# Three of the eleven down-projection chunks as split float32r products, and four other orders at the end of the gated MLP

## The chip, the cores and the metric

The kernel runs on one core of one Trainium2 chip. The metric is the device time of one execution in microseconds (us). Before the change three runs gave a median of 681.93 us (681.78 to 682.07).

## The reference, cut to what matters

Four residual layers run over x, 4 batches of 256 tokens of 512 values: attention, a mixture of experts (MoE), a gated MLP, and the same MoE once more. The change lies in the MLP and in what leads from it to the second MoE.

```python
s = silu(x @ w_gate.T)                          # 1024 x 1376
_, idx = top_k(-abs(s), 688)                    # the smaller half of each row ...
s = s.at[rows, idx].set(0.0)                    # ... becomes zero
x = x + (s * (x @ w_up.T)) @ w_down.T           # "down": 1376 -> 512

# MoE: a router, two of three experts for each batch
ratio = mean(abs(h[:, 76:])) / (mean(abs(h[:, :76])) + 1e-8)
scores = softmax(concat([h, ratio]) @ gate_w + gate_b)
# experts are chosen by a batch's first token; each has w1, a function, w2
```

## The kernel before, in words

The tokens lie in T = 8 tiles of 128. Matrix products of float32 accuracy are mostly made of three float32r products: each factor is split into a high part (cast to F32R) and a low part (the rest), and high·high, high·low and low·high are summed in PSUM. The transposes, `down` and a few small products take plain float32 factors; each such product stands as two MATMUL records in the trace.

The order on each engine is that of the program, with semaphores in between (`need(engine, signal, step, k)` waits for the k-th event of a step). In the MLP, PE goes through iterations n = 0 to 7 (the loop at the end of the tensor block):

1. `up(n)`, 3 groups of columns of 12 products each (banks 3, 4, 5). After the first group comes `check(n)`, a product that counts the rows whose threshold search failed. It waits for DVE's search of tile n (`mlp.pick`) and for the add of tile n-1 (`mlp.y_add`), because its result lies in bank 7, the bank of `down`. In iteration T-3 = 5 `check` first issues `route_sums`, four small products for the router of the second MoE, on bank 7 too.
2. `turn_row(n+3)`, then `gate(n+2)` (36 products, banks 0 to 2).
3. `turn_product(n)`: 11 transposes of `mlp_prod` into banks 6, 4 and 3 (k = 0, 1, 2). Before k = 2 it waits for `mlp.prodT` 1, DVE's copy of k = 0.
4. `down(n)`: 11 chunks of 128 (the last of 96) rows of `w_down`, in bank 7, all float32.

In iteration 7 there is no gate; PE does `ffn_turn(ffn2, 0)` before `up(7)` and `ffn_front(ffn2, 0)` behind it. After `down(7)` it turns row 1 of the second MoE and runs `ffn_front(ffn2, 1)`: for each of two experts high·high, high·low, and then low·high, which waits for `hT_lo` from DVE (`ffn_low`).

DVE does in iteration n: `mlp_add(n-1)` (x += bank 7, then the norm's statistics); `keep_mask(n)`; `product(n)` (two parts into `mlp_prod`); `keep_product(n)` (copies bank by bank into `prodT`, lines 1627 to 1639); `search(n+1)`; router rows `logit_rows(n-1)`. The last iterations hold more: in T-3 the router's `take_sums`, `scores` and `ranks`; in T-2 two low parts of w1 (`weight_low`), `mlp_add(6)`, and the router's `weights` and `middle_weights`. After the loop come `mix` of tile 0, three low parts of w2 (`second_weights`), `mlp_add(7)`, and then `ffn_dve`, which begins with `ffn_low(ffn2, 1)`.

ACT computes silu, sizes and six counting passes per tile, and casts the high parts of w1 and w2. POOL computes the norms' factors and some low parts. In the trace w1 and w2 of the second MoE are both called `w_second`.

Of the kernel before, what the change touches and what calls it, by code (L numbers as in the profile page):

```python
# [162 lines left out]
def build(nc, x_in, w_attn, b_attn, w_proj, b_proj, w_gate, w_up, w_down,  # L163
# [26 lines left out]
    with ExitStack() as ctx:  # L190
# [26 lines left out]
        bias1 = sb("bias1", [P, E, D], BF16)  # L217
        bias_proj = sb("bias_proj", [P, D], BF16)
# [124 lines left out]
        assert at[0] <= arena + G_AT  # L343
        at[0] = past_hT
# [38 lines left out]
        assert at[0] <= arena + 2 * W  # L383
# [4 lines left out]
        def turned(n):  # L388
            if n % 3 == 2:
# [70 lines left out]
                         slow=sig("mlp_slow", SLOW), prodT_ps=sig("mlp_prodT_ps", 3), prodT=sig("mlp_prodT", 4),  # L460
# [7 lines left out]
        wg_end_high, wg_end_low = sem("wg_end_high"), sem("wg_end_low")  # L468
        out_done, first_silu, first_gate = sem("out_done"), sem("first_silu"), sem("first_gate")
# [284 lines left out]
        def _(act):  # L754
# [271 lines left out]
            second_weights(w2_second, 1)  # L1026
# [3 lines left out]
        def _(dve):  # L1030
# [521 lines left out]
            def keep_mask(n, then):  # L1552
# [4 lines left out]
                if then is not None:  # L1557
                    then()
# [84 lines left out]
            for c in range(KC):  # L1643
# [7 lines left out]
                                    ALU.subtract).then_inc(wu_low, 1)  # L1651
            router = Router(route2, 0, CHECK_BANK, 8)
            search(0)
            for n in range(T):
                if 1 <= n < T - 1:
                    mlp_add(n - 1)
                if n == T - 1:
                    ffn_low(ffn2, 0, HT_BANK)
                keep_mask(n, router.take_sums if n == T - 3 else None)
                product(n)  # L1660
                keep_product(n)
                if n == T - 2:
                    for e in range(1, E):
                        weight_low(w1_second, w1_high, w1_low, 1, e, e)
                if n + 1 < T:
                    search(n + 1)
                if n == T - 2:
                    mlp_add(n)
                if 1 <= n < T - 1:
                    logit_rows(route2, n - 1)  # L1670
                if n == T - 3:
                    router.scores()
                    router.ranks()
                elif n == T - 2:
                    router.weights()
                    router.middle_weights()
# [6 lines left out]
        def _(pe):  # L1683
# [479 lines left out]
```

## Time and profile before

| what | value |
|---|---|
| median of 3 runs | 681.93 us |
| the profiled execution, its own time | 681.57 us |
| its span, first to last instruction | 679.8 us |
| TensorE's granted clock over the span | 1.000 |
| PE busy | 641.1 us (94%) |
| DVE busy | 483.0 us (71%) |
| ACT busy | 343.7 us (51%) |
| POOL busy | 92.0 us (14%) |
| PE's share of the chain that ended last | 79% |
| the MLP's `up`, from its first product to the last `down` | about 366 to 576 us |

The table is of one profiled execution on the chip; the times are from its span's start. The 1.77 us between span and time lie before the first and behind the last instruction. In a timeline a row holds the start in us, the us from the first start to the last end of the merged instructions, engine, line, operation, output<-inputs, shapes and how many; in brackets the engine's idle time before it and what it waited for. A matmul's own duration is longer than the distance to the next one, since they are pipelined: what PE needs is read from start to start.

### The profile page before, as it was taken

The page shows a single profiled execution, that of the slowest core. Times are in us where ns is not written, and L with a number is a line of the kernel's source. Part 1 is how long each engine was busy: PE and PEld are TensorE (multiplying, and loading weights), DVE is VectorE, ACT ScalarE, POOL GpSimd, SP SyncE. Part 2 cuts the span into 40 slices and gives each one's busy share as a digit, 9 for nine tenths or more (in the row PEclk, how much of TensorE's full clock was granted, in tenths as well). Part 3 has the DMA queues.
Part 4 walks back from the last instruction along what each step waited for, and adds up shares of the span by engine and source line. Part 5 has one row for each costly group of instructions (what it writes and reads, how often), then busy time and mean ns, then how long its engine had stood idle before and what let it go on. Part 6 is the DMA issues. An engine that isn't in the chain of part 4 may idle for free.

```text
span 679.8 us, 10305 instructions
## 1 busy us (share of the span) xinstructions
PE 641.1 (94%) x3848; PEld 487.2 (72%) x3848; DVE 483.0 (71%) x921; ACT 343.7 (51%) x539; POOL 92.0 (14%) x185
## 2 busy tenths in 40 slices
PE   4878999999998999999999899999999999999997
PEld 4856678679676677887788576766857665788776
DVE  6755585796589889887697656365374898778556
ACT  5213544613633774522479997476483915434221
POOL 4411002102100121101042010000100350000000
PEclk9999999999999999999999999999999999999999
DMA  8395503322744331000161000000003106000000
GB/s 282 110 264 173 157 32 97 117 70 73 241 128 146 119 121 47 0 1 1 49 225 61 1 0 1 0 1 0 1 0 114 74 7 225 2 32 16 15 32 32
DMA packets 31908, 52.15 MB, mean 77 GB/s; under 512 B 3449, under 2 KB 17148, under 8 KB 30303
## 3 DMA queue, kind: packets, MB, share of 16 engines
q1 hardware_dynamic: 31282, 49.84, 22.6%
q10 hardware_dynamic: 576, 1.64, 1.0%
q8 instruction: 32, 0.52, 0.3%
q14 instruction: 18, 0.15, 0.1%
HBM read 42.87 MB, written 8.40 MB: 75 GB/s over the span
## 4 chain that ended last, share of the span: by engine, by line
PE 79%; DVE 12%; ACT 4%; DMA 1%; issue 1%; ACTq 1%; POOL 1%; SPq 0%; DVEq 0%; POOLq 0%
PE ps L2031 14%; PE ps L1900 13%; PE ps L1867 13%; PE ps L2100 10%; PE ps L1730 5%; DVE nmax L1099 3%; PE ps L1808 3%; PE ps L1746 2%; PE ps L1876 2%; PE ps L1798 2%; PE ps L1710 2%; DVE nmax L1096 2%; ACT sign_junk L988 1%; PE ps L1821 1%; PE ps L2089 1%
## 5 line engine op out<-in xcount | busy, mean ns | idle before, releaser
L2100 PE MATMUL ps<-wdT,prodT 128*128 128x512 f32 (+1 forms) x176 | 76.9, 592 | 0.0
L817 ACT ACTIVATE probsT<-ps 128x1536 f32<-128x1536 f32 x32 | 46.2, 1450 | 30.2 <-PE ps L1798 30.0
L2100 PEld LDWEIGHTS ps<-wdT,prodT 128*128 128x128 f32 (+1 forms) x176 | 32.8, 190 | 38.3 <-issue 38.3
L857 ACT ACTIVATE funs<-ps 128x512 f32<-128x512 f32 x16 | 9.5, 596 | 90.4 <-PE ps L1869 78.7
L683 POOL TENSOR_SCALAR ln_spread<-ln_moments 128x1 f32<-128x1 f32 x24 | 7.5, 311 | 272.1 <-DVE ln_moments L1171 271.9
L1633 DVE COPY prodT<-ps 128x512 f32<-128x512 f32 (+1 forms) x24 | 13.7, 599 | 41.3 <-PE ps L2089 41.0
L1177 DVE SCALAR_TENSOR_TENSOR junk<-x_sb,gate_row 128x512 f32<-128x512 f32 x48 | 41.2, 858 | 1.0
L1448 DVE SCALAR_TENSOR_TENSOR x_sb<-b_row,coef,x_sb 128x512 f32<-128x512 f32 x48 | 38.0, 792 | 1.8
L1099 DVE TENSOR_REDUCE nmax<-ps 128x4 f32<-128x1024 f32 x32 | 38.9, 1215 | 0.0
L988 ACT ACTIVATE sign_junk<-mlp_size_next,minus_guess 128x1376 bf16<-128x1376 f32 x24 | 34.6, 1443 | 0.8
L988 ACT ACTIVATE sign_junk<-mlp_size_main,minus_guess 128x1376 bf16<-128x1376 f32 x24 | 34.6, 1442 | 0.7
L918 ACT CAST aT_hi<-ps 128x512 fp32r<-128x512 f32 x32 | 17.2, 591 | 34.2 <-PE ps L1876 34.2
L676 POOL TENSOR_TENSOR parts<-resid,parts 128x512 bf16<-128x512 f32 x16 | 18.7, 1173 | 101.2 <-ACT parts L792 101.2
L785 ACT ACTIVATE parts<-ps,qk_bias 128x256 bf16<-128x256 f32 x32 | 13.4, 468 | 35.4 <-PE ps L1730 35.4
L1376 DVE TENSOR_TENSOR aT_lo<-ps,aT_hi 128x512 fp32r<-128x512 f32 x32 | 20.6, 684 | 12.7 <-ACT aT_hi L918 12.6
L1086 DVE SCALAR_TENSOR_TENSOR resid<-ps,qk_bias,parts 128x256 f32<-128x256 f32 x32 | 14.0, 479 | 21.8 <-ACT parts L785 21.8
L1128 DVE COPY outT<-ps 128x256 f32<-128x256 f32 x32 | 13.5, 423 | 22.4 <-PE ps L1813 22.4
L1798 PE MATMUL ps<-qst,kst 107*128 107x256 bf16 x128 | 24.5, 272 | 0.0
L1769 PE MATMUL ps<-kst,qst 104*128 104x256 bf16 x128 | 24.5, 272 | 0.0
L1730 PE MATMUL ps<-rowsT_hi,wqkv_hi 128*128 128x256 f32 x128 | 22.4, 299 | 2.1 <-DVE rowsT_lo L1053 1.4
L1457 DVE TENSOR_TENSOR x_sb<-ps,x_sb 128x512 f32<-128x512 f32 x16 | 11.1, 691 | 18.6 <-PE ps L1900 18.5
L1808 PE MATMUL ps<-probsT,v_ones 128*32 128x256 f32 x256 | 20.4, 391 | 3.7 <-DVE o_tok L1122 2.6
(302 smaller groups left out, 1726.4 us busy)
## 6 DMA issues: line engine op xcount, KB each, us to landing
cuts<-parts SPq DMA_DIRECT2D x16, 384.0 KB, 2.8
qst<-cuts SPq DMA_DIRECT2D x48, 128.0 KB, 2.6
w_first_raw<-in_L_ffn_w SPq DMA_DIRECT2D x6, 1024.0 KB, 7.6
w_second_raw<-in_L_ffn_w SPq DMA_DIRECT2D x6, 1024.0 KB, 8.5
kst<-cuts SPq DMA_DIRECT2D x36, 128.0 KB, 2.8
wqkv_raw<-in_L_attn_a_w_attn SPq DMA_DIRECT2D x3, 1024.0 KB, 8.0
wdT<-in_L_attn_b_w_down SPq DMA_DIRECT2D x1, 2560.0 KB, 9.9
wg_raw<-in_L_attn_b_w_gate SPq DMA_DIRECT2D x1, 2048.0 KB, 8.4
```

What stands on the lines that cost most here:

```text
L817: nc.scalar.activation(probsT[:, g % 2, :].rearrange("p (k n) -> p k n", k=3), slot[g % 2], ACT.Exp).then_inc(exp_ok.sem, 1)
L988: nc.scalar.activation(sign_junk[:, :], size_rows(n)[1][:, :], ACT.Sign, bias=minus_guess[:, i:i + 1], accum_out=probe_sum[:, i:i + 1]).th ...
L1099: nc.vector.tensor_reduce(nmax[:, 1, g * G:(g + 1) * G], sl[:, 1:3, :].rearrange("p s (h k) -> p (s h) k", h=2), AX.X, ALU.max, negate=Tru ...
L1177: nc.vector.scalar_tensor_tensor(out=junk[:, :], in0=x_sb[:, t, :], scalar=1.0, in1=gate_v[:, 0:D, e], op0=ALU.mult, op1=ALU.mult, accum_o ...
L1448: nc.vector.scalar_tensor_tensor(out=x, in0=b2_row[:, e, :], scalar=coef[:, n, e:e + 1], in1=x, op0=ALU.mult, op1=ALU.add).then_inc(ffn.b2 ...
L1730: last = nc.tensor.matmul(turn_bank(b, f)[:, m * S:(m + 1) * S], weight[:, side, c, columns], rows[:, c, :], start=(i == 0 and c == 0), st ...
L1798: m = nc.tensor.matmul(sl[:, 1 + i // 2, (i % 2) * S:(i % 2 + 1) * S], kst[0:MROWS, h, 0:P], qst[0:MROWS, h, :], start=False, stop=True, s ...
L1808: nc.tensor.matmul(o_ps[32 * i:32 * i + 2 * HD, 0:S], v_ones[:, 0, h, :], probsT[:, g % 2, D + i * S:D + (i + 1) * S], start=True, stop=Fa ...
L1867: nc.tensor.matmul(ps[:, 2 * i + s, :], a[:, i, c, :], part[:, e, c, :], start=(k == 0 and c == 0), stop=False)
L1900: last = nc.tensor.matmul(ps[:, Y_BANK, :], a[:, s, c, :], part[:, e[s], c, :], start=(k == 0 and c == 0), stop=(k == len(products) - 1 an ...
L2031: last = nc.tensor.matmul(ps[:, first_bank + q, 0:m], a[:, c, :], parts_of[c][part], start=(k == 0 and c == 0), stop=(k == 2 and c == KC - 1))
L2100: last = nc.tensor.matmul(ps[:, Y_BANK, :], prodT[0:m, c, :], wdT[0:m, c, :], start=(c == 0), stop=(c == IC - 1))
```

## The change

- **Down.** Chunks 5, 6 and 7 of 11 become three float32r products each: `prodT_hi`·`wd_hi`, `prodT_hi`·`wd_lo`, `prodT_low`·`wd_hi`. DVE splits the weights once, before `search(0)` (1536 columns). In every tile it splits the product: one cast and two subtractions in `split_product`, and the copy of bank 4 shrinks to chunk 4. The order of `down` becomes chunks 0 to 3, then 5 to 7, then 4, then 8 to 10.
- **The transposes' wait.** `turn_product` waits before k = 2 for `mlp.prod` 2 (both parts of the product) in place of `mlp.prodT` 1.
- **The router's sums** leave `check` and come behind `up(5)`, ahead of `gate(7)`. DVE takes them, and does `scores` and `ranks`, between `product(5)` and `keep_product(5)`.
- **DVE's end.** In iteration 6 the two low parts of w1 come behind `search(7)`, with `mlp_add(6)` between them; `logit_rows(5)` moves into iteration 7, ahead of `keep_product(7)`; `weights` and `middle_weights` come after `keep_product(7)`.
- **ACT** waits for `wd_read` (`down(7)`'s last float32r product) before the cast of w2's third expert, whose place `wd_hi` uses.

```diff
+        prodT_hi = sb("prodT_hi", [P, NSPLIT, P], F32R, prodT_at + 4 * SPLIT.start * P)
+        wd_at = arena + LATE + W - 4 * IC * D
+        wdT = sb("wdT", [P, IC, D], F32, wd_at)
+        wd_lo = sb("wd_lo", [P, NSPLIT, D], F32R, wd_at + 4 * SPLIT.start * D)
+        wd_hi = sb("wd_hi", [P, NSPLIT, D], F32R, wd_at - 4 * NSPLIT * D)
...
-            second_weights(w2_second, 1)
+            second_weights(w2_second, 1, range(E - 1))
+            act.wait_ge(wd_read, 1)
+            second_weights(w2_second, 1, (E - 1,))
...
+            def split_product(n, chunks_ps):
+                nc.vector.tensor_copy(prodT_hi[:, :, :], chunks_ps).then_inc(mlp.prodT.sem, 1)
+                need(dve, mlp.prodT, n, 2)
+                for low, part in zip(prodT_low, (slice(0, NSPLIT - 1), slice(NSPLIT - 1, NSPLIT))):
+                    nc.vector.tensor_tensor(low[:, :, :], chunks_ps[:, part, :], prodT_hi[:, part, :].bitcast(F32),
+                                            ALU.subtract).then_inc(mlp.prodT.sem, 1)
...
+                    if k == 1:
+                        split_product(n, turned_ps[:, SPLIT.start - 4:SPLIT.stop - 4, :])
+                        chunks = SPLIT.start - 4
...
+            dve.wait_ge(wd_here, 32)
+            nc.vector.tensor_copy(wd_hi[:, :, :], wdT[:, SPLIT, :]).then_inc(wd_high, 1)
+            dve.wait_ge(wd_high, 1)
+            nc.vector.tensor_tensor(wd_lo[:, :, :], wdT[:, SPLIT, :], wd_hi[:, :, :].bitcast(F32),
+                                    ALU.subtract).then_inc(wd_low, 1)
...
-                keep_mask(n, router.take_sums if n == T - 3 else None)
+                keep_mask(n)
                 product(n)
+                if n == T - 3:
+                    router.take_sums()
+                    router.scores()
+                    router.ranks()
+                elif n == T - 1:
+                    logit_rows(route2, T - 3)
                 keep_product(n)
-                if n == T - 2:
-                    for e in range(1, E):
-                        weight_low(w1_second, w1_high, w1_low, 1, e, e)
                 if n + 1 < T:
                     search(n + 1)
-                if n == T - 2:
+                if 1 <= n < T - 2:
+                    logit_rows(route2, n - 1)
+                elif n == T - 2:
+                    weight_low(w1_second, w1_high, w1_low, 1, 1, 1)
                     mlp_add(n)
-                if 1 <= n < T - 1:
-                    logit_rows(route2, n - 1)
-                if n == T - 3:
-                    router.scores()
-                    router.ranks()
-                elif n == T - 2:
-                    router.weights()
-                    router.middle_weights()
+                    weight_low(w1_second, w1_high, w1_low, 1, 2, 2)
+            router.weights()
+            router.middle_weights()
             mix(ffn2, route2, 0, 0)
...
-                if n == T - 3:
-                    route_sums(route2, 0, CHECK_BANK, 8)
...
-                        need(pe, mlp.prodT, n, 1)
+                        need(pe, mlp.prod, n, 2)
...
-                for c in range(IC):
+                for c in range(4):
+                    if c == 0:
+                        need(pe, mlp.prodT, n, 1)
+                    nc.tensor.matmul(ps[:, Y_BANK, :], prodT[:, c, :], wdT[:, c, :], start=(c == 0), stop=False)
+                if n == 0:
+                    pe.wait_ge(wd_low, 1)
+                need(pe, mlp.prodT, n, 4)
+                for k in range(NSPLIT):
+                    high, low = prodT_hi[:, k, :], prodT_low[k // (NSPLIT - 1)][:, k % (NSPLIT - 1), :]
+                    for a, w in ((high, wd_hi), (high, wd_lo), (low, wd_hi)):
+                        last = nc.tensor.matmul(ps[:, Y_BANK, :], a, w[:, k, :], start=False, stop=False)
+                if n == T - 1:
+                    last.then_inc(wd_read, 1)
+                for c in [*range(4, SPLIT.start), *range(SPLIT.stop, IC)]:
...
                 up(n)
+                if n == T - 3:
+                    need(pe, mlp.mask, n, 1)
+                    route_sums(route2, 0, CHECK_BANK, 8)
```

PE at the end of a tile, here of tile 4 (`mlp_prod` is transposed, then `down`). Before:

```order
L2089 MATMUL ps<-ident,mlp_prod 128x128 x10
L2089 MATMUL ps<-ident,mlp_prod 96x128
L2100 MATMUL ps<-wdT,prodT 128x512 x11
L2031 MATMUL ps<-wu_hi,hT_hi_third 128x512 x4
L2031 MATMUL ps<-wu_lo,hT_hi_third 128x512 x4
L2031 MATMUL ps<-wu_hi,hT_lo_third 128x512 x4
```

With the change (`prodT_low_162` and `prodT_low_175` are the two low parts of the product; "..." leaves out a triple that reads as the one above it):

```order
L2118 MATMUL ps<-ident,mlp_prod 128x128 x10
L2118 MATMUL ps<-ident,mlp_prod 96x128
L2126 MATMUL ps<-wdT,prodT 128x512 x4
L2133 MATMUL ps<-wd_hi,prodT_hi 128x512
L2133 MATMUL ps<-wd_lo,prodT_hi 128x512
L2133 MATMUL ps<-wd_hi,prodT_low_162 128x512
...
L2133 MATMUL ps<-wd_hi,prodT_hi 128x512
L2133 MATMUL ps<-wd_lo,prodT_hi 128x512
L2133 MATMUL ps<-wd_hi,prodT_low_175 128x512
L2144 MATMUL ps<-wdT,prodT 128x512 x4
```

Seven float32 chunks are left of eleven, and nine float32r products stand between chunk 3 and chunk 4.

PE in `up(5)`, behind its first group of columns. Before:

```order
L2031 MATMUL ps<-wu_hi,hT_lo_third 128x512 x4
L1832 MATMUL ps<-abs_n,vision 128x2
L1833 MATMUL ps<-abs_n,text 128x2
L1835 MATMUL ps<-abs_n,ones_78 128x2
L1837 MATMUL ps<-logits_n,first_row 128x6
L2067 MATMUL ps<-ones_78,failed 1x1
L2031 MATMUL ps<-wu_hi,hT_hi_third 128x512 x4
L2031 MATMUL ps<-wu_lo,hT_hi_third 128x512 x4
L2031 MATMUL ps<-wu_hi,hT_lo_third 128x512 x4
```

With the change:

```order
L2062 MATMUL ps<-wu_hi,hT_lo_third 128x512 x4
L2096 MATMUL ps<-ones_78,failed 1x1
L2062 MATMUL ps<-wu_hi,hT_hi_third 128x512 x4
L2062 MATMUL ps<-wu_lo,hT_hi_third 128x512 x4
L2062 MATMUL ps<-wu_hi,hT_lo_third 128x512 x4
L2062 MATMUL ps<-wu_end_hi,hT_hi_third 128x352 x4
L2062 MATMUL ps<-wu_end_lo,hT_hi_third 128x352 x4
L2062 MATMUL ps<-wu_end_hi,hT_lo_third 128x352 x4
L1863 MATMUL ps<-abs_n,vision 128x2
L1864 MATMUL ps<-abs_n,text 128x2
L1866 MATMUL ps<-abs_n,ones_78 128x2
L1868 MATMUL ps<-logits_n,first_row 128x6
```

The four products of the router (`abs_n`, `logits_n`) now follow the last product of `up` and precede `gate(7)`; `check` (`failed`) follows the first group directly.

DVE from the last copy of tile 7 into the second MoE. Before:

```order
L1638 COPY prodT<-ps 96x128
L1421 TENSOR_SCALAR funs<-funs,coef_mid 128x512
L1424 SCALAR_TENSOR_TENSOR act_tok<-funs,coef 128x512
L1382 TENSOR_TENSOR w_second_lo<-w_second_raw,w_second_hi 128x2048 x3
L1623 TENSOR_TENSOR x_sb<-ps,x_sb 128x512
L1169 BN_STATS ln_stats<-x_sb 128x6
L1171 BN_AGGR ln_moments<-ln_stats 128x2
L1376 TENSOR_TENSOR hT_lo<-ps,hT_hi 128x512
```

With the change ("..." leaves out eleven more instructions of the router's `weights`):

```order
L1663 COPY prodT<-ps 96x128
L1360 TENSOR_REDUCE tiny<-tiny 128x4
...
L1385 TENSOR_TENSOR coef<-coef,tiny 128x12
L1387 TENSOR_TENSOR coef_mid<-coef,tiny 128x4 x2
L1390 TENSOR_SCALAR coef_half<-coef 128x4
L1438 TENSOR_SCALAR funs<-funs,coef_mid 128x512
L1441 SCALAR_TENSOR_TENSOR act_tok<-funs,coef 128x512
L1399 TENSOR_TENSOR w_second_lo<-w_second_raw,w_second_hi 128x2048 x3
L1638 TENSOR_TENSOR x_sb<-ps,x_sb 128x512
L1186 BN_STATS ln_stats<-x_sb 128x6
L1188 BN_AGGR ln_moments<-ln_stats 128x2
L1393 TENSOR_TENSOR hT_lo<-ps,hT_hi 128x512
```

The router's weights stand behind the last copies and ahead of the mix, the low parts of w2, the last add and `hT_lo` of row 1.

## Rows read from the trace of the kernel before

**Rows 1.** The chain that ended last on the page, its shares of the span by line
```profile
PE ps L2031 14%; PE ps L1900 13%; PE ps L1867 13%; PE ps L2100 10%; PE ps L1730 5%; DVE nmax L1099 3%; PE ps L1808 3%; PE ps L1746 2%; PE ps L1876 2%; PE ps L1798 2%; PE ps L1710 2%; DVE nmax L1096 2%; ACT sign_junk L988 1%; PE ps L1821 1%; PE ps L2089 1%
```

**Rows 2.** Timeline of PE, tile 1's product turned, its down, up of tile 2: start us, us, instructions
```profile
410.92 1.04 PE L2089 MATMUL ps<-ident,mlp_prod 128*128 128x128 f32 x8
412.31 0.55 PE L2089 MATMUL ps<-ident,mlp_prod 128*128 128x128 f32 x3 [0.35 <-DVE prodT L1633]
412.69 9.61 PE L2100 MATMUL ps<-wdT,prodT 128*128 128x512 f32 x22
...
423.07 1.07 PE L2031 MATMUL ps<-wu_lo,hT_hi_third 128*128 128x512 f32 x4
423.97 1.07 PE L2031 MATMUL ps<-wu_hi,hT_lo_third 128*128 128x512 f32 x4
424.97 0.19 PE L2067 MATMUL ps<-ones,failed 128*1 128x1 f32 x2
...
426.13 1.08 PE L2031 MATMUL ps<-wu_lo,hT_hi_third 128*128 128x512 f32 x4
```

**Rows 3.** Timeline of DVE in the same stretch
```profile
411.56 1.75 DVE L1633 COPY prodT<-ps 128x512 f32<-128x512 f32 x3 [7.86 <-PE ps L2089]
...
413.43 0.14 DVE L1538 TENSOR_SCALAR ladder<-minus_guess 128x1 f32<-128x1 f32 x1
...
421.88 0.09 DVE L1177 DVE_READ_ACCUMULATOR junk<-x_sb,gate_row 128x1 f32 x1
422.33 0.69 DVE L1623 TENSOR_TENSOR x_sb<-ps,x_sb 128x512 f32<-128x512 f32 x1 [0.37 <-PE ps L2100]
...
430.10 0.52 DVE L1574 TENSOR_TENSOR mlp_prod<-mlp_s_next,ps 128x352 f32<-128x352 f32 x1 [0.61 <-PE ps L2031]
```

**Rows 4.** Timeline of DVE before the first search
```profile
373.08 0.15 DVE L1538 TENSOR_SCALAR ladder<-minus_guess 128x1 f32<-128x1 f32 x1 [4.78 <-ACT sign_junk L988]
```

**Rows 5.** The tile wdT: its first load (issue at us) and both loads' times to landing
```profile
L613 SPq DMA_DIRECT2D wdT<-in_L_attn_b_w_down x1: 368/368/368, 350.0 to 350.0; - x1
...
DMA to landing us min/median/max: 9.9/10.0/10.1
```

**Rows 6.** Timeline of PE, up of tile T-3 = 5
```profile
504.74 1.07 PE L2031 MATMUL ps<-wu_hi,hT_lo_third 128*128 128x512 f32 x4
506.53 0.35 PE L1832 MATMUL ps<-abs_n,vision 128*128 128x2 f32 x2 [0.72 <-POOL logits_n L700]
...
507.49 0.19 PE L2067 MATMUL ps<-ones,failed 128*1 128x1 f32 x2
```

**Rows 7.** Timeline of PE, up of tile T-2 = 6, and its down's start
```profile
532.97 1.07 PE L2031 MATMUL ps<-wu_hi,hT_lo 128*128 128x512 f32 x4
534.35 0.19 PE L2067 MATMUL ps<-ones,failed 128*1 128x1 f32 x2 [0.32 <-DVE x_sb L1623]
...
541.29 9.61 PE L2100 MATMUL ps<-wdT,prodT 128*128 128x512 f32 x22
```

**Rows 8.** Timeline of DVE, tiles 6 and 7 into the second MoE
```profile
556.99 0.15 DVE L1343 TENSOR_REDUCE tiny<-tiny 128x4 f32<-128x12 f32 x1
...
559.32 0.68 DVE L1376 TENSOR_TENSOR hT_lo<-ps,hT_hi 128x512 fp32r<-128x512 f32 x1
...
567.51 0.47 DVE L1421 TENSOR_SCALAR funs<-funs,coef_mid 128x512 f32<-128x512 f32 x1
...
568.68 2.28 DVE L1382 TENSOR_TENSOR w_second_lo<-w_second_raw,w_second_hi 128x2048 fp32r<-128x2048 f32 x1
...
576.41 0.69 DVE L1623 TENSOR_TENSOR x_sb<-ps,x_sb 128x512 f32<-128x512 f32 x1 [0.15 <-PE ps L2100]
...
577.97 0.66 DVE L1376 TENSOR_TENSOR hT_lo<-ps,hT_hi 128x512 fp32r<-128x512 f32 x1
```

**Rows 9.** Timeline of ACT, the third cast of the second w2
```profile
572.04 1.90 ACT L845 CAST w_second_hi<-w_second_raw 128x2048 fp32r<-128x2048 f32 x1 [0.76 <-DMA w_second_raw<-in_L_ffn_w]
```

**Rows 10.** Timeline of PE, second MoE, front of tile 1, its third product
```profile
579.45 1.10 PE L1867 MATMUL ps<-w_second_hi,hT_lo 128*128 x4
```

More of the change, by code:

```diff
@@ L217, in build @@
         bias1 = sb("bias1", [P, E, D], BF16)
+        bias_proj_at = at[0]
         bias_proj = sb("bias_proj", [P, D], BF16)
@@ L343, in build @@
         assert at[0] <= arena + G_AT
+        SPLIT = slice(5, 8)
+        NSPLIT = SPLIT.stop - SPLIT.start
         at[0] = past_hT
@@ L350, in build @@
         mlp_flag = sb("mlp_flag", [P, I], BF16)
+        prodT_at = at[0]
         prodT = sb("prodT", [P, IC, P], F32)
+        prodT_hi = sb("prodT_hi", [P, NSPLIT, P], F32R, prodT_at + 4 * SPLIT.start * P)
+        prodT_low = [sb("prodT_low0", [P, NSPLIT - 1, P], F32R)]
         assert at[0] <= arena + G_AT, at[0] - arena - G_AT
@@ L368, in build @@
         wu_end_hi = sb("wu_end_hi", [P, KC, IT], F32R, b2_at)
+        prodT_low.append(sb("prodT_low1", [P, 1, P], F32R, bias_proj_at))
         wu_hi = sb("wu_hi", wide_shape, F32R, arena + W)
-        wdT = sb("wdT", [P, IC, D], F32, arena + LATE)
+        wd_at = arena + LATE + W - 4 * IC * D
+        wdT = sb("wdT", [P, IC, D], F32, wd_at)
+        wd_lo = sb("wd_lo", [P, NSPLIT, D], F32R, wd_at + 4 * SPLIT.start * D)
+        wd_hi = sb("wd_hi", [P, NSPLIT, D], F32R, wd_at - 4 * NSPLIT * D)
+        assert SPLIT.start > 4 and SPLIT.stop == 8
         assert MAIN + TAIL + 4 * IT <= W and 4 * IC * D <= W and TAIL <= 4 * E * D
@@ L382, in build @@
         hT_lo_third = sb("hT_lo_third", [P, KC, P], F32R)
-        assert at[0] <= arena + 2 * W
+        assert at[0] <= wd_at - 4 * NSPLIT * D
         def size_rows(n):
@@ L459, in build @@
                          pick=sig("mlp_pick", 7), check=sig("mlp_check", 1), mask=sig("mlp_mask", 2), prod=sig("mlp_prod", 2),
-                         slow=sig("mlp_slow", SLOW), prodT_ps=sig("mlp_prodT_ps", 3), prodT=sig("mlp_prodT", 4),
+                         slow=sig("mlp_slow", SLOW), prodT_ps=sig("mlp_prodT_ps", 3), prodT=sig("mlp_prodT", 7),
                          y_ps=sig("mlp_y_ps", 1), y_add=sig("mlp_y_add", 1))
@@ L468, in build @@
         wg_end_high, wg_end_low = sem("wg_end_high"), sem("wg_end_low")
+        wd_high, wd_low, wd_read = sem("wd_high"), sem("wd_low"), sem("wd_read")
         out_done, first_silu, first_gate = sem("out_done"), sem("first_silu"), sem("first_gate")
@@ L1550, in search, with keep_mask @@
                 link(nc.vector.tensor_scalar(failed[:, :], cut_count[:, :], float(KEEP), None, ALU.not_equal))
-            def keep_mask(n, then):
+            def keep_mask(n):
                 rows, size = size_rows(n)
@@ L1556, in keep_mask @@
                 nc.vector.tensor_copy(failures[0:1, :], check_ps).then_inc(mlp.mask.sem, 1)
-                if then is not None:
-                    then()
                 need(dve, mlp.mask, n, 1)
@@ L1632, in keep_product @@
                         chunks -= 1
-                    nc.vector.tensor_copy(prodT[:, 4 * k:4 * k + chunks, :],
-                                          ps[:, PROD_BANK[k], 0:chunks * P].rearrange("p (c t) -> p c t", t=P)
+                    turned_ps = ps[:, PROD_BANK[k], :].rearrange("p (c t) -> p c t", t=P)
+                    if k == 1:
+                        split_product(n, turned_ps[:, SPLIT.start - 4:SPLIT.stop - 4, :])
+                        chunks = SPLIT.start - 4
+                    nc.vector.tensor_copy(prodT[:, 4 * k:4 * k + chunks, :], turned_ps[:, 0:chunks, :]
                                           ).then_inc(mlp.prodT.sem, 1)
@@ L2093, in down @@
             def down(n):
-                for c in range(IC):
+                for c in range(4):
[12 more added lines that the diff above has]
+                for c in [*range(4, SPLIT.start), *range(SPLIT.stop, IC)]:
                     m = min(P, I - c * P)
-                    if c % 4 == 0:
-                        need(pe, mlp.prodT, n, c // 4 + 1)
+                    if c == 4:
+                        need(pe, mlp.prodT, n, 5)
+                    elif c == SPLIT.stop:
+                        need(pe, mlp.prodT, n, 6)
                     elif c == IC - 1:
-                        need(pe, mlp.prodT, n, 4)
+                        need(pe, mlp.prodT, n, 7)
                     last = nc.tensor.matmul(ps[:, Y_BANK, :], prodT[0:m, c, :], wdT[0:m, c, :],
-                                            start=(c == 0), stop=(c == IC - 1))
+                                            start=False, stop=(c == IC - 1))
                 last.then_inc(mlp.y_ps.sem, 1)
```

## The prediction

> **What bounds the kernel now.** I read the page's chain first: PE's lines lead it, and L2031 (`up` and `gate`), L2100 (`down`) and L2089 (the transposes) are 25% of the span [rows 1]. So the MLP is timed by PE, and the questions are how much PE time goes, and whether another engine then comes late. For that I went through PE's timeline tile by tile, then DVE's beside it, then ACT and the loads where a wait is added. PE does not stand still in a middle tile but for two gaps: one inside the transposes, for DVE's copy [rows 2], and one of about 0.1 us ahead of `check`.
>
> **1. Down, three chunks in float32r.** A float32 chunk is two passes. From the first pass of `down` at 412.69 to the `wu_lo` products at 423.07 lie 22 passes and four float32r products [rows 2]. Four of those take 0.90 us (423.07 to 423.97), 0.225 each. So 10.38 - 0.90 = 9.48 us for 22 passes: 0.43 each, 0.86 a chunk. Three chunks cost 2.58 us, nine float32r products 2.03 to 2.07. Saved: **0.52 us a tile**. The switch from float32 to float32r inside that stretch leaves nothing over; the switch back I also take at nothing.
>
> The Trainium skill, page "TensorE: Matmul & The Clock Gate", section "Back-to-back issue gap", gives a sustained 131 ns for each 512-column matmul in a stream with weight loads. This trace has 225. By the page nine products would be 1.18 us and the saving 1.40 a tile; I go by the row.
>
> **2. The transposes' wait.** Before, PE waits at 412.31 for the copy of k = 0, then does three transposes, and `down` starts at 412.69 [rows 2]. After, these three fill the gap: eight transposes take 0.87 (11 in all about 1.2 us, to 412.1), and `down` starts when the same copy is there, at 412.31. Saved: 412.69 - 412.31 = **0.38 us a tile**. `mlp.prod` 2 has long come: DVE makes it before PE's 36 products of `gate`.
>
> So a tile is 0.90 us shorter. That holds for tiles 0 to 5 and 7: 7 x 0.90 = **6.3 us**.
>
> **3. DVE's additional work in each tile.** Before, `keep_product` takes 413.43 - 411.56 = 1.87 us with four instructions [rows 3]. After there are seven: widths 512, 384, 256, 128, 128, 256, 128. A one-column operation takes 0.14 [rows 3], a 512-column one from PSUM 0.66 [rows 8], so 0.14 + 0.001 a column: the four new pieces (384, 256, 128, 128) are 0.53 + 0.40 + 0.27 + 0.27 less the 0.66 that goes, some 0.07 less for each overlap, 0.05 more for the wait of the low parts on the cast: **+0.65 us**. Bounds: +0.4 (the columns alone), and +2.9, if each of the four took 0.69 and a wait of its own. I take 0.65, since the copies in the same rows show the overlap.
>
> Is it covered? Count from the first copy, S = 411.56. DVE is free of its router rows at 421.97 = S + 10.4 [rows 3]; then it adds (0.69), which `check` waits for. After: S + 11.05 + 0.7 = S + 11.8. PE issued `check` at 424.97 = S + 13.4 [rows 2], after at S + 12.5. 0.7 us are left, so nothing is lost in tiles 2 to 6. PE reaches chunk 5 some 3.4 us into `down`, when the split (S + 1.8) has been over for 2 us or more.
>
> The split of the weights (1536 columns, at most two operations of 1.7 us by the 2.28 of a 2048-column one [rows 8]) stands ahead of `search(0)`, where DVE idles for 4.78 us waiting for ACT [rows 4]. Its data, issued at 350.0, land 10 us later [rows 5], before that idle time starts at 368.3. Cost 0; without this cover it would be up to 3.4 us, once.
>
> **4. The router's sums.** Before, the last products ahead of `check` in tile 5 start at 504.74, so `check` could go at 505.74 (1.00 us later, as 423.97 to 424.97 [rows 2]); it goes at 507.49, having waited 0.72 us for POOL and issued four small products [rows 6]: 1.75 us lost. After, POOL has been done for some 3 us when PE comes to them, and they cost 507.49 - 506.53 = 0.96 plus 0.1 to start. DVE's scores and ranks fall into its idle time before the transposes (7.86 us in such a tile [rows 3]). Saved: **0.7 us** (bounds 0.5 and 0.9).
>
> **5. Tile 6.** `check(6)` waited for the add of tile 5, as DVE was late with scores and ranks: it went at 534.35 and could have gone at 532.97 + 1.00 = 533.97 [rows 7]. Saved 0.38. From `check` to `down` were 541.29 - 534.35 = 6.94 us, as there is no `gate` between. After: DVE's second part of the product starts 430.10 - 424.97 = 5.13 us after a `check` [rows 2, 3], 0.44 later comes the copy of k = 0 (0.69), then `down`: 6.3 us. Saved 0.6. With the 0.52 of part 1: **1.5 us**.
>
> **6. The end of DVE, a new wait.** From S = 567.51 - 1.87 = 565.64, tile 7's first copy, DVE now does: `keep_product` 1.87 + 0.65 = 2.5; the router's weights 559.32 - 556.99 = 2.3; the mix 568.68 - 567.51 = 1.2; three low parts of w2 at 2.28 each, 6.8; the add and statistics 577.97 - 576.41 = 1.6; `hT_lo` of row 1, 0.66 [rows 8]. Its end: S + 15.1. Before, PE used `hT_lo` at 579.45 = S + 13.8 [rows 10]; with PE 0.90 ahead it wants it at S + 12.9. So **PE waits 2.1 us**, in order, in `ffn_front(ffn2, 1)`, and nothing behind it makes that up. Bounds: 1.3 (the low parts overlap, the rest is short) and 3.0 (the split costs more).
>
> ACT's wait for `wd_read`: the third cast starts at 572.04 and waited for its load until then [rows 9]. `down(7)` passes its last float32r product 0.69 + 3.4 + 2.1 = 6.2 us after S, at 571.9 in the old times: level with the load, cost 0 to 0.3 on ACT, covered by DVE's other low parts.
>
> In tile 6 DVE does only one low part of w1 ahead of the add instead of two; PE's `check(7)` finds the add done about 1 us earlier. 0.
>
> **Sum:** 6.3 + 0.7 + 1.5 - 2.1 = 6.4 us. From the profiled execution's 681.57: 675.2. The median of the runs is 0.36 above that execution; I predict **675.5 us**, its own range 674.5 to 676.6. A measurement of this kernel tells about 0.2% (1.4 us) from no change.
>
> **Rivals.**
> - **No wait at the end** (or a short one): the 2.1 us rest on a sum of DVE pieces. If they overlap more, or PE gets to `ffn_front(ffn2, 1)` later, the whole 8.5 us stay: 673.4. Against it: the router's 2.3 us are new in this row of work, and before it DVE had only 0.8 us to spare.
> - **Switches between float32 and float32r cost.** `check` is two float32 passes among float32r ones: 423.97 to 426.13 is 2.16 us for eight products, 1.80 without it [rows 2]. Some 0.3 us, of which the passes are 0.05. `down` gets one more pair of switches a tile: at most 8 x 0.25 = 2.0 us, 677.5. Against it: the wait for a semaphore explains part, and the first switch in part 1 shows none.
> - **DVE becomes the bound, slower.** `check(n)` waits for the add, the add for DVE's row of copies, search and router rows. Past +1.35 us (0.65 + 0.7) each further us counts in five to six tiles and again at the end. At the bound of +2.9 that is 1.55 x 6 = 9.3 and 2.3 at the end: 675.5 + 11.6 = 687. It decides for slower from about +2.5 on. For it: four more instructions, each with a fixed part. Against it: the overlap in rows 3.
> - **Products at half the distance.** Were two float32r products to overlap as they stream, each would take half of the 0.225 of rows 2; the nine would be 1.0 us and 1.0 us a tile more would go: 675.5 - 8.1 = 667.4. Every float32r product of 512 columns in this trace speaks against it. The rule of the Trainium skill in part 1 is of this kind.
>
> **How the numbers follow.** Forecast 0.68; no or a short wait at the end 0.13; switches 0.12; DVE as the bound 0.03; half the distance 0.01; something unseen that takes most of the gain 0.03. The range of 8 in 10 takes in the second and most of the third: 673.2 to 677.4. Faster by over 0.2%: all but the fourth and the last, 0.94; within 0.2%: 0.03; slower: 0.03.
>
> **What would show it.** In the timeline of PE after: the transposes x11 without idle time; nine products at 0.23 us between the float32 passes; `down` 0.5 us shorter; tile to tile 26.0 instead of 26.9 us; no wait at `check(6)`; and, in the front of row 1 of the second MoE, an idle time of about 2 us ahead of its third product, released by DVE `hT_lo`. Wrong would be: a wait of `check` for `x_sb` in tiles 2 to 5, float32 passes that start late behind the float32r ones, or no idle time at `hT_lo`.

## The result and the profile after

| | before | after |
|---|---|---|
| median of the runs | 682.00 us (681.78 to 683.65, 6 runs) | 676.70 us (676.22 to 679.00, 6 runs) |
| ratio, 95% interval | | 0.9921 (0.9904 to 0.9937) |
| the profiled execution | 681.57 us, span 679.8 | 678.16 us, span 676.4 |
| granted clock over its span | 1.000 | 0.995 |

The kernel is 5.3 us faster. The forecast was 675.5 us, its range 673.2 to 677.4. The one execution of the six whose granted clock was 1.000 took 676.22 us; the profiled one spent two stretches at a lower clock (one in the attention stage, one in the second MoE), and the trace lets us take the second out.

Timeline of PE after, tile 1, the place of [rows 2]:

```profile
410.55 1.36 PE L2118 MATMUL ps<-ident,mlp_prod 128*128 128x128 f32 x11
411.93 3.70 PE L2126 MATMUL ps<-wdT,prodT 128*128 128x512 f32 x8
415.07 0.80 PE L2133 MATMUL ps<-wd_hi,prodT_hi 128*128 128x512 f32 x1
415.70 0.40 PE L2133 MATMUL ps<-wd_lo,prodT_hi 128*128 128x512 f32 x1
...
417.34 0.40 PE L2133 MATMUL ps<-wd_hi,prodT_low 128*128 128x512 f32 x1
417.57 3.60 PE L2144 MATMUL ps<-wdT,prodT 128*128 128x512 f32 x8
420.61 1.49 PE L2062 MATMUL ps<-wu_hi,hT_hi_third 128*128 128x512 f32 x4
421.94 1.07 PE L2062 MATMUL ps<-wu_lo,hT_hi_third 128*128 128x512 f32 x4
...
423.84 0.19 PE L2096 MATMUL ps<-ones,failed 128*1 128x1 f32 x2
```

The transposes stand as x11 with no idle time, and the float32r products follow one another at 0.234 us (415.70 to 417.34, seven steps). From the first transpose to `wu_lo` it is 421.94 - 410.55 = 11.39 us; before it was 423.07 - 410.92 = 12.15 [rows 2]. A tile is 0.76 us shorter, not 0.90.

Timeline of DVE after, the same tile:

```profile
411.18 0.69 DVE L1659 COPY prodT<-ps 128x512 f32<-128x512 f32 x1 [7.86 <-PE ps L2118]
411.79 0.55 DVE L1643 CAST prodT_hi<-ps 128x384 fp32r<-128x384 f32 x1
412.37 0.62 DVE L1646 TENSOR_TENSOR prodT_low<-ps,prodT_hi 128x256 fp32r<-128x256 f32 x2
...
413.64 0.14 DVE L1555 TENSOR_SCALAR ladder<-minus_guess 128x1 f32<-128x1 f32 x1
...
422.07 0.68 DVE L1638 TENSOR_TENSOR x_sb<-ps,x_sb 128x512 f32<-128x512 f32 x1
```

`keep_product` takes 413.64 - 411.18 = 2.46 us, 0.59 more than the 1.87 of [rows 3]. The add ends at 422.75, `check` is issued at 423.84: it waits for nothing, with 1.1 us to spare.

PE in tiles 5 and 6, the places of [rows 6] and [rows 7]:

```profile
501.35 1.07 PE L2062 MATMUL ps<-wu_hi,hT_lo_third 128*128 128x512 f32 x4
502.35 0.19 PE L2096 MATMUL ps<-ones,failed 128*1 128x1 f32 x2
...
507.29 0.28 PE L1863 MATMUL ps<-abs_n,vision 128*128 128x2 f32 x2
...
508.09 1.18 PE L2062 MATMUL ps<-wg_hi,hT_hi 128*128 128x512 f32 x4
...
529.00 0.19 PE L2096 MATMUL ps<-ones,failed 128*1 128x1 f32 x2
...
535.32 1.13 PE L2126 MATMUL ps<-wdT,prodT 128*128 128x512 f32 x2
```

Both checks go 1.00 us behind the group ahead of them (in tile 6 that group starts at 528.00); the router's products cost 0.80 us at 507.29, with no wait for POOL; `down(6)` begins 6.32 us after `check(6)`.

PE behind `down(7)`, the place of [rows 10]:

```profile
569.12 0.60 PE L1877 MATMUL ps<-ident,h_cur 128*128 128x128 f32 x4
570.39 1.20 PE L1898 MATMUL ps<-w_second_hi,hT_hi 128*128 x4 [0.68 <-ACT hT_hi L864]
571.43 1.09 PE L1898 MATMUL ps<-w_second_lo,hT_hi 128*128 x4
574.32 1.20 PE L1898 MATMUL ps<-w_second_hi,hT_lo 128*128 x4 [1.79 <-DVE hT_lo L1393]
...
575.40 2.02 PE L1898 MATMUL ps<-w_second_hi,hT_hi 128*128 x4
577.22 1.91 PE L1898 MATMUL ps<-w_second_lo,hT_hi 128*128 x4
578.93 1.17 PE L1898 MATMUL ps<-w_second_hi,hT_lo 128*128 x4
...
580.17 1.04 PE L1907 MATMUL ps<-ident,act_tok 128*128 128x128 f32 x8
```

The predicted wait is there: the third group starts 2.89 us after the second, where it was 0.93. But two groups behind it need 1.82 and 1.71 us in place of 1.13 and 0.92. The windows of PE show why (stretch, its length, PE busy, the granted clock, DMA):

```profile
574.30:575.40 1.10, 1.08 (x5) 1.00 0.00 0
575.40:578.90 3.50, 3.50 (x10) 0.54 0.00 0
578.90:582.40 3.50, 3.50 (x21) 0.97 0.00 0
...
575.60:575.70 0.10, 0.10 (x2) 0.88 0.00 0
...
579.00:579.10 0.10, 0.10 (x2) 0.55 0.00 0
```

The granted clock fell to half (of the two levels, 1.2 GHz) at 575.7, 1.4 us after PE had resumed at 574.32, and came back at 579.0, some 3.4 us later. DVE's end, for [rows 8]:

```profile
559.29 0.69 DVE L1659 COPY prodT<-ps 128x512 f32<-128x512 f32 x1 [2.27 <-PE ps L2118]
...
565.45 6.69 DVE L1399 TENSOR_TENSOR w_second_lo<-w_second_raw,w_second_hi 128x2048 fp32r<-128x2048 f32 x3
572.06 0.69 DVE L1638 TENSOR_TENSOR x_sb<-ps,x_sb 128x512 f32<-128x512 f32 x1
...
573.61 0.66 DVE L1393 TENSOR_TENSOR hT_lo<-ps,hT_hi 128x512 fp32r<-128x512 f32 x1
```

From the first copy (S = 559.29) to `hT_lo` the timeline marks no idle time of DVE.

**Where the 3.4 us between the two spans come from.** Three marks in each PE timeline: the first transpose of tile 0's product (384.00 before, 384.37 after), that of tile 7's (565.00, 558.65) and the first transpose of `act_tok` (583.64, 580.17).

| stretch | before | after | difference |
|---|---|---|---|
| span's start to tile 0's transposes | 384.00 | 384.37 | +0.37 |
| to tile 7's transposes | 181.00 | 174.28 | -6.72 |
| `down(7)`, to the transposes of row 1 | 11.22 | 10.47 | -0.75 |
| row 1's front, to `act_tok` | 7.42 | 11.05 | +3.63 |
| to the end of the span | 96.16 | 96.23 | +0.07 |

The +3.63 are 9.50 - 7.42 = 2.08 for the wait and 11.05 - 9.50 = 1.55 for the low clock: in another execution of the same code (r_after, below), whose groups behind the wait keep their usual distances, this stretch is 9.50 us.

### The profile page after: what moved, and what is told of

Read it like the earlier page. It is cut to its first block, busy times and chain, and to the rows that moved or that the text cites. A ratio compares the mean times of both kernels' runs of the same rounds, so it can differ in the third digit from the quotient of the medians.

```text
span 676.4 us, 10382 instructions
## 1 busy us (share of the span) xinstructions
PE 640.8 (95%) x3872; PEld 493.7 (73%) x3872; DVE 490.3 (72%) x947; ACT 343.9 (51%) x539; POOL 89.2 (13%) x185
## 3 DMA queue, kind: packets, MB, share of 16 engines
q10 hardware_dynamic: 576, 1.64, 1.1%
## 4 chain that ended last, share of the span: by engine, by line
PE 79%; DVE 12%; ACT 4%; DMA 2%; ACTq 1%; issue 1%; POOL 1%; SPq 0%; DVEq 0%
PE ps L2062 15%; PE ps L1931 13%; PE ps L1898 13%; PE ps L2126 4%; PE ps L1761 4%; PE ps L2144 4%; DVE nmax L1116 3%; PE ps L1839 3%; PE ps L1777 2%; PE ps L2133 2%; PE ps L1907 2%; PE ps L1829 2%; PE ps L1741 2%; DVE nmax L1113 2%; ACT sign_junk L1003 1%; PE ps L2118 1%
## 5 line engine op out<-in xcount | busy, mean ns | idle before, releaser
L698 POOL TENSOR_SCALAR ln_spread<-ln_moments 128x1 f32<-128x1 f32 x24 | 9.0, 373 | 271.4 <-DVE ln_moments L1188 271.3
L1659 DVE COPY prodT<-ps 128x512 f32<-128x512 f32 (+2 forms) x24 | 10.4, 462 | 39.4 <-PE ps L2118 39.4
L2126 PE MATMUL ps<-wdT,prodT 128*128 128x512 f32 x64 | 29.6, 605 | 0.2
L2144 PE MATMUL ps<-wdT,prodT 128*128 128x512 f32 (+1 forms) x64 | 28.8, 592 | 0.0
```

What stands on the lines that cost most here:

```text
L2126: nc.tensor.matmul(ps[:, Y_BANK, :], prodT[:, c, :], wdT[:, c, :], start=(c == 0), stop=False)
```

## The experiments

The yardstick is the **MLP stretch**, from the first transpose of tile 0's product to that of `act_tok`, read in each profile, beside the **tile period**, from one tile's first transpose to the next (median of the first four). They leave out the attention stage, whose clock differs from execution to execution.

| kernel | median us | ratio to before | tile period | MLP stretch |
|---|---|---|---|---|
| before | 682.00 | | 26.92 | 199.64 |
| after | 676.70 | 0.9921 (0.9904 to 0.9937) | 26.17 | 195.80 (1.6 of it low clock) |
| e1_wait | 680.99 | 0.9981 (0.9972 to 0.9990) | 26.64 | 198.52 |
| e2_orders | 679.75 | 0.9961 (0.9947 to 0.9975) | 26.64 | 196.78 |
| e3_end | 674.96 | 0.9895 (0.9880 to 0.9911) | 26.17 | 192.16 |
| e4_last | 678.12 | 0.9942 (0.9928 to 0.9955) | 26.15 | 194.10 |
| r_after | 678.07 | 0.9943 (0.9929 to 0.9957) | 26.17 | 194.23 |
| r_end | 675.21 | 0.9891 (0.9876 to 0.9906) | 26.17 | 192.17 |
| e9_turn | 673.64 | 0.9882 (0.9864 to 0.9899) | 26.17 | 191.42 |
| e8_dve4 | 691.69 | 1.0138 (1.0116 to 1.0160) | 28.2 | 208.46 |
| e6_two | 677.91 | 0.9932 (0.9909 to 0.9954) | 26.32 | 195.17 |
| e7_dve1 | 676.65 | 0.9920 (0.9897 to 0.9943) | 26.17 | 194.22 |
| e10_route | 678.78 | 0.9950 (0.9932 to 0.9968) | 26.17 | 195.88 |

Rows e1 to e4, r_after to e8, and e6 to e10 are three sets on chips of their own, where the kernel before took 682.46, 681.89 and 681.89 us. The ratio of a row is to the kernel before on its own chip.

**The transposes' wait alone, in the kernel before.**

```diff
-                        need(pe, mlp.prodT, n, 1)
+                        need(pe, mlp.prod, n, 2)
```

> The kernel before, with only the transposes' wait changed (mlp.prod 2 instead of mlp.prodT 1). Theory: the last three transposes fill the 0.38 us between the copy being asked for and being there, in each of 8 tiles: 682.0 - 3.0 = 679.0 us, and the transposes stand as x11 without idle time. Rival: the wait only moves ahead of the first product of down, which waits for the same copy: 682.0 us.

Measured: the stretch is 1.12 us shorter, not 3.0. PE at tile 1, and the checks of tiles 6 and 7:

```profile
411.07 1.36 PE L2089 MATMUL ps<-ident,mlp_prod 128*128 128x128 f32 x11
412.45 9.71 PE L2100 MATMUL ps<-wdT,prodT 128*128 128x512 f32 x22
...
533.24 0.19 PE L2067 MATMUL ps<-ones,failed 128*1 128x1 f32 x2 [0.48 <-DVE x_sb L1623]
...
553.66 0.19 PE L2067 MATMUL ps<-ones,failed 128*1 128x1 f32 x2 [0.96 <-DVE x_sb L1623]
```

`down` starts 1.38 us behind the first transpose instead of 1.77, as predicted, but then takes 0.10 longer: in tile 7 it is 9.54 us to the next transposes where it was 9.45. So the period shrinks by 0.28, not 0.38. And 1.1 of the 2.2 us that eight tiles bring are lost at once to DVE, which is late with the adds of tiles 5 and 6: `check(7)` waits 0.96 us where it did not wait before. The other orders of the change are what cashes the gain (next run).

**The orders without the split.** All eleven chunks in float32, no `split_product`, no split of the weights.

```diff
-                need(pe, mlp.prodT, n, 4)
-                for k in range(NSPLIT):
-                    high, low = prodT_hi[:, k, :], prodT_low[k // (NSPLIT - 1)][:, k % (NSPLIT - 1), :]
-                    for a, w in ((high, wd_hi), (high, wd_lo), (low, wd_hi)):
...
+                for c in range(IC):
+                    m = min(P, I - c * P)
+                    if c % 4 == 0:
+                        need(pe, mlp.prodT, n, c // 4 + 1)
```

> The changed kernel with all eleven chunks of down in float32 and no split; the orders and the transposes' wait stay. Theory: in the trace of the changed kernel the split takes 9.08 us per down where it was 9.45, so 0.37 us a tile and 3.0 in all come back. At the end of the MLP DVE has 0.6 us less to do and PE arrives 0.37 later, so the wait for hT_lo shrinks from 1.96 to about 1.0: 676.7 + 3.0 - 1.0 = 678.7 us; 677.2 if the 1.5 us lost to the lower clock behind that wait go too. Rival (the term as predicted, 0.52 a tile): 676.7 + 4.2 - 1.1 = 679.8 us.

Measured: a period of 26.64, so three split chunks save 26.64 - 26.17 = **0.47 us a tile**, between the theory's 0.37 and the 0.52 of the prediction. (The 0.37 came from comparing `down` with that of before, whose transposes end earlier.) The wait for `hT_lo` is shorter, as expected:

```profile
575.78 1.10 PE L1888 MATMUL ps<-w_second_lo,hT_hi 128*128 x4
577.49 1.20 PE L1888 MATMUL ps<-w_second_hi,hT_lo 128*128 x4 [0.60 <-DVE hT_lo L1391]
```

It costs 8.31 - 7.42 = 0.89 us. Against the changed kernel the stretch is 2.55 us longer (194.23 to 196.78): 8 x 0.47 = 3.76 come back, 1.18 of wait go. Against e1_wait the orders alone, of the router and of DVE together, are worth 198.52 - 196.78 = 1.74 us.

**DVE's end in another order** (and once more as r_end, beside the changed kernel as r_after).

```diff
-            second_weights(w2_second, 1)
+            for e in range(E - 1):
+                weight_low(w2_second, w2_high, w2_low, 1, e, e)
             mlp_add(T - 1)
+            ffn_low(ffn2, 1, HT_BANK)
+            weight_low(w2_second, w2_high, w2_low, 1, E - 1, E - 1)
```

> The changed kernel with hT_lo of row 1 and the last add ahead of the third low part of w2 on DVE. Theory: the wait of 1.96 us for hT_lo goes, and with it the stretch at the lower clock behind it, which cost 1.5 us in the profiled run: 676.7 - 3.5 = 673.2 us. If the lower clock has nothing to do with the idle time: 674.7 us, and the stretch is still to be seen in some runs. Rival: another wait takes its place in row 1 or 2 of the second MoE (the mix of row 1 or the third low part comes late): 676.7 us.

> The changed kernel with hT_lo of row 1 and the last add ahead of the third low part of w2, once more, beside the changed kernel on the same chip. Theory: 2.1 us of wait are gone, 674.6 us against 676.7; and if the lower clock behind the wait is a consequence of the wait, fewer of its runs than of the changed kernel's have a clock below 0.997. Rival: the difference on the first chip was the chip, and here it is under 1 us.

> The changed kernel once more, for a time beside the next three on one chip. All theories: 676.7 us, 676.2 where the granted clock stays 1.000, with a wait of 1.8 us for hT_lo in row 1.

Measured: the stretch is 192.16 and 192.17 against 194.23, 2.07 us less. The wait is gone and nothing took its place:

```profile
571.50 1.08 PE L1901 MATMUL ps<-w_second_lo,hT_hi 128*128 x4
572.43 1.09 PE L1901 MATMUL ps<-w_second_hi,hT_lo 128*128 x4
```

On the one chip the medians differ by 678.07 - 675.21 = 2.9 us. So the wait cost 2.07 us, and the time it cost was on the path. The part on the clock is not settled: in 2 of the 4 runs of r_end and in 4 of the 5 of r_after the mean clock was below 0.997, which is too few to tell them apart.

The expectation for r_after failed: its median is 678.07 us, not 676.7. Its one execution at a mean clock of 0.997 took 676.60, the four at 0.995 or 0.992 took 678.04 to 678.76. The profiles show what such a mean is made of: no stretch at the lower level at 1.000, one at 0.997 (in the attention stage in all of them), two at 0.995 (`after`), three at 0.993 (e8_dve4). So the median of one and the same kernel moves by over 1 us with the share of its executions in which the clock falls more than once. The MLP stretch of a single profile does not have this spread.

**The float32r products last.** In tiles 0 to 6, chunks 0 to 4 and 8 to 10 first, then the nine products, right ahead of `up`.

```diff
+                    singles(rest)
+                    last = triples()
```

> The changed kernel with the nine float32r products at the end of down (tiles 0 to 6), right ahead of up's float32r products, so that one pair of switches between float32 and float32r a tile goes. Theory: the switches cost the 0.1 us a tile that is left when nine products at 0.233 and eight passes at 0.43 are taken from the measured stretch: 676.7 - 0.7 = 676.0 us. Rival 1, switches are free: 676.7 us. Rival 2, a switch costs the 0.4 us that the first product behind the float32 passes stands longer in the trace: 676.7 - 2.8 = 673.9 us.

Measured: a period of 26.15 against 26.17. One pair of switches a tile fewer brings 0.02 us, not the theory's 0.1 and not the 0.4 of rival 2: **the switches cost nothing that shows**.

```profile
418.29 0.80 PE L2140 MATMUL ps<-wd_hi,prodT_hi 128*128 128x512 f32 x1
418.93 0.39 PE L2140 MATMUL ps<-wd_lo,prodT_hi 128*128 128x512 f32 x1
...
420.79 1.08 PE L2062 MATMUL ps<-wu_hi,hT_hi_third 128*128 128x512 f32 x4
421.70 1.07 PE L2062 MATMUL ps<-wu_lo,hT_hi_third 128*128 128x512 f32 x4
```

The `wu_hi` group now takes 0.91 us instead of 1.33, but the eight passes that were between the products and it have only moved ahead of them. So the extra 0.4 us of a first float32r product (0.63 in tile 1's rows, 0.64 here) is no loss; most likely it is recorded while the float32 pass ahead of it still runs. The median of 678.12 says nothing against it; its five executions had mean clocks of 1.000 (676.26 us), 0.995 (three) and 0.992 (679.15).

**Two split chunks instead of three.**

```diff
-        SPLIT = slice(5, 8)
+        SPLIT = slice(6, 8)
```

> The changed kernel with two split chunks (6 and 7) instead of three. The trace gives 26.64 us a tile without a split and 26.17 with three chunks. Theory (a gain per chunk, no fixed price of the switches): two thirds of 0.47, so 26.33 us a tile, 0.16 x 8 = 1.3 us less gain, of which DVE's shorter work (0.13) and PE's later arrival (0.16) give 0.3 back at the end: 677.7 us. Rival (a fixed price of 0.1 us a tile in each down, 0.19 us a chunk): 26.36 us a tile.

Measured: a period of 26.32. Each split chunk is worth 0.16 us (0.32 for two, 0.47 for three), and a fixed part, if there is one, is within the 0.02 to 0.03 us that rounding leaves.

**More work on DVE**, by one and by four idle reductions in each of tiles 0 to 5:

```diff
+                    for k in range(4):
+                        dve.wait_ge(spare_ok, 4 * n + k)
+                        nc.vector.tensor_reduce(spare[:, 0:4], x_sb[:, T - 1, :].rearrange("p (a b) -> p a b", a=4), AX.X,
+                                                ALU.add).then_inc(spare_ok, 1)
```

> The changed kernel with one idle reduction of 512 columns more on DVE in each of tiles 0 to 5, 0.7 us a tile. Theory (1.0 us to spare ahead of check): nothing, 26.17 us a tile and the time of the changed kernel, 676.7 us. Rival (every us on DVE in this row counts): 26.9 us a tile, 681 us.

> The changed kernel with four idle reductions of 512 columns more on DVE in each of tiles 0 to 5, about 2.6 us a tile. Theory (check waits for the add, with 1.0 us to spare in the trace of the changed kernel): checks 2 to 6 wait 1.6 us each for x_sb, 8 us in all: 684.7 us, and tile 1 waits for nothing, as it has no router rows. Rival (DVE's row has more slack than the add shows): 676.7 us.

Measured: one (0.69 us of record, 0.6 in the row of work) costs nothing, the period stays at 26.17. Four make every check of tiles 1 to 6 wait. PE in tile 3, and its clock there:

```profile
455.72 0.19 PE L2103 MATMUL ps<-ones,failed 128*1 128x1 f32 x2 [1.72 <-DVE x_sb L1640]
...
456.88 1.51 PE L2069 MATMUL ps<-wu_lo,hT_hi 128*128 128x512 f32 x4
458.18 1.91 PE L2069 MATMUL ps<-wu_hi,hT_lo 128*128 128x512 f32 x4
```

```profile
455.70:457.00 1.30, 1.28 (x7) 1.00 0.05 13
457.00:460.50 3.50, 3.50 (x12) 0.55 0.00 0
```

The four move the router rows by 2.76 us and the undisturbed period grows by 27.93 - 26.17 = 1.76: if each us past the reserve counts in full, the reserve is **1.0 us**. The timeline of the changed kernel gives the same by itself: 1.1 us between the end of the add and `check`. The expected 8 us became 14.2. Tile 1 waits too (its period grows by 1.9): it has no router rows, but its search starts late, behind a wait of 2.60 us for ACT. Behind two of the six waits the clock fell to the lower level, 1.6 us each time. And the five expected waits lengthen their periods by 1.75 to 2.07 us each instead of 1.6, which is the last 1.1.

**The router's products back ahead of `check(5)`.**

```diff
+                if n == T - 3:
+                    route_sums(route2, 0, CHECK_BANK, 8)
                 nc.tensor.matmul(check_ps, failed[:, :], ones32[:, 0:1], start=True, stop=True,
...
-                    need(pe, mlp.mask, n, 1)
-                    route_sums(route2, 0, CHECK_BANK, 8)
```

> The changed kernel with the router's four products back ahead of check(5); DVE's order stays as changed. Theory (the predicted term of 0.7 us for POOL's late logits_n): 0.7 to 0.8 us more in tile 5, whose period is 26.64 us now: 27.4 us and 677.4 us in all. Rival (POOL is no longer late in this order, or DVE's order made the gain): 26.64 us and 676.7.

Measured: tile 5 takes 28.29 us instead of 26.65, 1.64 more, and the stretch 195.88 against 194.22 (e7_dve1, whose period is that of the changed kernel, on the same chip).

```profile
501.06 1.07 PE L2062 MATMUL ps<-wu_hi,hT_lo_third 128*128 128x512 f32 x4
503.69 0.35 PE L1863 MATMUL ps<-abs_n,vision 128*128 128x2 f32 x2 [1.56 <-POOL logits_n L715]
```

The direction is the theory's, the size twice it. PE could now issue them at 502.06 (1.00 behind the group at 501.06) where it was 505.74 before, 3.7 us earlier; POOL is only 2.8 us earlier (503.69 against 506.53 [rows 6]), so the wait has grown from 0.72 to 1.56. Without this move 0.84 of the 3.7 us gained by then would have been given back here.

**Row 1's transposes inside `down(7)`**, on top of e3_end, and `hT_lo` ahead of the last add. Bank 6 is free there, since `down` itself waited for DVE's copy of it.

```diff
+                    if n == T - 1 and c == SPLIT.stop:
+                        ffn_turn(ffn2, 1, HT_BANK)
```

> As the run before this one, and the four transposes of row 1 stand inside the last down, ahead of chunk 8, with hT_lo ahead of the last add. Theory: PE waits 0.68 us for ACT's cast of hT_hi behind these transposes in every kernel so far; with 1.3 us of down behind them the cast is hidden: 0.7 us less than the run before. Rival: hT_lo or the functions of row 0 on ACT come late in its place: no difference.

Measured: 0.75 us less in the stretch (191.42), and the timeline marks no idle time of PE any more between tile 0's transposes and `act_tok`:

```profile
566.49 0.60 PE L1880 MATMUL ps<-ident,h_cur 128*128 128x128 f32 x4
566.92 2.74 PE L2149 MATMUL ps<-wdT,prodT 128*128 128x512 f32 x6
569.62 1.17 PE L1901 MATMUL ps<-w_second_hi,hT_hi 128*128 x4
...
571.56 1.10 PE L1901 MATMUL ps<-w_second_hi,hT_lo 128*128 x4
```

At 673.64 us this kernel is below both r_end (675.21) and the changed kernel (r_after, 4.4 us more) on the same chip.

## Why the prediction was right, and where it was off

| step of the prediction | predicted | measured |
|---|---|---|
| 1. down, three chunks in float32r | 0.52 a tile | 0.47 (e2_orders against after) |
| 2. the transposes' wait | 0.38 a tile | 0.28 (e1_wait against before) |
| both, tiles 0 to 5 and 7 | 6.3 | 7 x 0.75 = 5.25 |
| 3. DVE's additional work | +0.65, hidden | +0.59, hidden; 1.0 in reserve |
| 4. the router's sums | 0.7 | 1.30 - 0.47 = 0.83 (excess of tile 5's period) |
| 5. tile 6 | 1.5 | 1.39 (what is left of its two periods) |
| 6. the wait for `hT_lo` | 2.1 | 2.07 |
| sum | 6.4 | 5.4 |

The measured 5.4 are the stretch's 199.64 - 194.23. From the 681.57 us of the profiled execution they lead to 676.2, and the run at clock 1.000 took 676.22. So every mechanism was there. The saving was put 1.0 us too high, and 1.05 of that is in one place, with small ones beside it that nearly cancel.

**The step that failed is the pair 1 and 2**, 0.75 us a tile instead of 0.90. In part 2 I took what `down` starts earlier for what is saved. But when all eleven transposes run directly ahead of `down`, its 22 passes take 9.55 us to the next work, not 9.45 (e1_wait, e2_orders). That the transposes' end and `down`'s start overlap is the likely reason, but only argued; the 0.10 is measured. In part 1 nine products take 9 x 0.234 = 2.10 us where I had 2.03 to 2.07, which is most of the missing 0.05. By the rule of the Trainium skill, page "TensorE: Matmul & The Clock Gate", section "Back-to-back issue gap" (131 ns for a 512-column product in a stream with weight loads), the saving would have been 1.40 a tile, an estimate; the traces differ from it, with 0.234 us for such a product and 0.47 a tile.

**Tile 6** is 0.11 below its term. Its two waits gave what was predicted: 0.38, since `check(6)` now goes 1.00 us behind its group instead of 1.38, and 0.62, since `down(6)` begins 6.32 us behind it instead of 6.94. The 0.10 of the transposes is the likely rest. **The router's term** was larger by 0.13; e10_route shows that by itself it is not a constant: it is worth 0.83 against the kernel before and 1.64 inside the change.

**The wait at the end** came out at 2.07, and not by luck: from S to the end of `hT_lo` are 574.27 - 559.29 = 14.98 us (15.1 in the sum), and PE wanted it at S + 13.07 (12.9), 0.93 behind its second group. Of the pieces of the sum none is off by more than 0.2: the router's weights took 2.5 (2.3 predicted), the three low parts of w2 6.6 (6.8). The two ends give 1.91 and the groups' distance 1.96; the remaining 0.1 of the 2.07 is lost behind the wait, and no run shows where. ACT's wait for `wd_read` cost nothing, as its cast at 566.99 waited 2.13 us for the load.

**The rivals.** No wait at the end: fell, the wait was there. Costly switches: fell, by e4_last and e6_two. DVE as the bound: its price was right in kind (e8_dve4), but it starts from a dose of 1.0 us beyond the changed kernel's work, and the change stays below. Products at half the distance: fell, 0.234 us each.

**What I did not foresee** is the clock. In the profiled execution it fell behind the wait, and with this 1.6 us and 0.4 more ahead of the MLP the execution gained only 3.4 us. That the wait brought it about is not shown.

**Where luck had a part.** That the median fell inside the range also rests on how seldom the clock fell in these six executions, of which two had a mean below 0.997. The same kernel on another chip (r_after, four of five below 0.997) had a median of 678.07 us, 3.8 us below the kernel before there (681.89) and above the range of 673.2 to 677.4. The range had no term for this.

## What to carry to other kernels

Read the worth of a removed wait from start to start over a whole period, not from the start of the next instruction; here 0.38 was 0.28. Price every wait against the state after the other parts (the router's was worth 0.83 us before and 1.64 inside the change): a part that makes PE earlier makes each producer that stays where it is (POOL's `logits_n`, DVE's adds and `hT_lo`) later in comparison, so that orders which save little alone decide how much of the gain arrives. And when work is added to an engine's closing row, look for what in it is needed last: one low part of w2, ready at 572 us and not used before 585, stood ahead of `hT_lo`. With that part behind it (e3_end, r_end) the 2.07 us came back.

## What the runs showed of the hardware

The granted clock fell to its lower level in the middle of steady work, shortly after PE had stood still for 1.7 to 1.8 us: once in the profile of the changed kernel and twice in that of e8_dve4, 1.1 to 1.6 us after PE had resumed, for some 3.4 us, at a price of about 1.6 us each. It did not do so behind waits of the same length in the profiles of r_after, e4_last, e7_dve1 and e10_route, nor behind the five other waits of 1.7 to 2.0 us of e8_dve4. So such a wait doesn't always bring it about, and how often it does, and whether a kernel without the wait is spared, stays open: runs with a mean clock of 0.995 occur in the kernel before and in e9_turn too, and in the profiles that have such a stretch elsewhere it lies at the start of the attention stage (between 33 and 52 us), where PE stands idle for a sixth to a third of the time.

Nine float32r products put between float32 passes cost nothing beyond their own 0.234 us each: with one pair of switches a tile fewer the period changed by 0.02 us (e4_last).
